# Float16 halves for three sets of float32 products, and a new order of items, in a fused AdaLN layer

## The reference

```
h = layernorm(x) * (1 + ca) + sa
x = x + ga * attn(h)     # rmsnorm, in_w, gate; two branches:
                         #   a: 4-tap depthwise conv, two low-rank maps (A, Bm), ha
                         #   b: 9-tap depthwise conv, silu, pw, hb
                         #   y = gate * fuse([a, b]); out_w; + residual
h = layernorm(x) * (1 + cb) + sb
x = x + gb * moe(h)      # 160 experts of width 64, top 8 by sigmoid, plus a shared expert
shared = silu(h @ w_gate_shared.T) @ w_down_shared.T
```

## Time and profile before

| | us |
|---|---|
| Median of 3 runs | 523.34 (523.1 to 523.37) |
| Profiled execution | 523.24 |
| its span | 521.5 |
| PE busy | 506.1 (97%) |
| DVE busy | 493.2 (95%) |
| ACT busy | 422.2 (81%) |
| POOL busy | 24.9 (5%) |

### The profile page before, as it was taken

How to read it: one execution, slowest core, us unless ns; L and a number is a source line. 1 busy time by engine, 2 the same in 40 slices (tenths; PEclk the granted TensorE clock), 3 DMA queues, 4 the chain that set the end, 5 groups by cost and what they waited for, 6 DMA issues and landing times.

```text
span 521.5 us, 7182 instructions
## 1 busy us (share of the span) xinstructions
PE 506.1 (97%) x2416; PEld 244.3 (47%) x2416; DVE 493.2 (95%) x637; ACT 422.2 (81%) x690; POOL 24.9 (5%) x45
## 2 busy tenths in 40 slices
PE   7897899999999999999999999999999999999996
PEld 5543444544454444444554444444454444444442
DVE  6999999999999999999999999998999989999995
ACT  6588998889989977877999877884799877877773
POOL 6211001001000000000200000000100000000000
PEclk9998999999999999999999999999999999999999
DMA  7797364556664765565354656564465766666650
GB/s 267 256 366 294 128 216 166 162 173 203 194 190 155 239 190 196 183 215 178 129 195 147 239 179 203 188 212 140 162 202 160 223 205 206 204 207 205 209 165 20
DMA packets 33165, 101.30 MB, mean 194 GB/s; under 512 B 3684, under 2 KB 8936, under 8 KB 33128
## 3 DMA queue, kind: packets, MB, share of 16 engines
q1 hardware_dynamic: 33128, 100.84, 58.9%
...
## 4 chain that ended last, share of the span: by engine, by line
PE 87%; DVE 5%; ACT 2%; DMA 2%; issue 2%; SPq 1%; ACTq 0%; DVEq 0%
PE bank L1158 27%; PE bank L1159 27%; PE bank L1160 27%; PE bank L1304 2%; DMA idf<-idf_dram 1%; PE bank L1314 1%; DMA mod<-rows_mod 1%; DVE w L953 1%; PE bank L1403 1%; SPq L551 0%; PE bank L1169 0%; ACT s_all L809 0%; PE bank L1426 0%; PE bank L1324 0%; PE bank L1201 0%
## 5 line engine op out<-in xcount | busy, mean ns | idle before, releaser
L809 ACT ACTIVATE s_all<-bank 128x512 f32<-128x512 f32 x320 | 188.9, 594 | 70.3 <-PE bank L1160 69.0
L1118 DVE TENSOR_TENSOR g_all<-s_all,g_all 128x1024 f16<-128x1024 f32 x160 | 195.7, 1223 | 13.6 <-ACT g_all L828 13.3
L1129 DVE TENSOR_TENSOR s_all<-s_all,c_all 128x1024 f32<-128x1024 f32 x158 | 193.1, 1222 | 0.0
L828 ACT ACTIVATE g_all<-s_all 128x1024 f16<-128x1024 f32 x160 | 168.2, 1051 | 1.1 <-DVE s_all L1129 1.1
L1158 PE MATMUL bank<-g_all,w 128*128 128x512 f16 x320 | 121.3, 379 | 0.7 <-DVE g_all L1118 0.7
L1158 PE MATMUL bank<-x_h,w 128*128 128x512 f16 x320 | 121.3, 379 | 0.6 <-ACT s_all L809 0.5
L1159 PE MATMUL bank<-g_all,w 128*128 128x512 f16 x320 | 121.3, 379 | 0.0
L1160 PE MATMUL bank<-g_all,w 128*128 128x512 f16 x320 | 121.3, 379 | 0.0
L1160 PE MATMUL bank<-x_l,w 128*128 128x512 f16 x320 | 121.3, 379 | 0.0
L1159 PE MATMUL bank<-x_h,w 128*128 128x512 f16 x320 | 121.3, 379 | 0.0
L1158 PEld LDWEIGHTS bank<-g_all,w 128*128 128x128 f16 x320 | 31.3, 98 | 40.0 <-DVE g_all L1118 2.8
...
## 6 DMA issues: line engine op xcount, KB each, us to landing
...
```

The source lines that it names most:

```text
L809: a(sr[J % SRING][:, q * L:(q + 1) * L], U[q][:], ACT.Silu, scale=1.0 / ES).then_inc(s["s_done"], 1)
L828: a(gh[n % GRING], sr[n % SRING], ACT.Copy).then_inc(s["hi_set"], 1)
L1118: e.tensor_tensor(gl[n % GRING], sr[n % SRING], gh[n % GRING], ALU.subtract).then_inc(s["lo_set"], 1)
L1129: e.tensor_tensor(sr[J % SRING], sr[J % SRING], cr[J % CRING], ALU.mult).then_inc(s["gm"], 1)
```

## The change

Three things are changed.

1. The shared down product takes float16 pairs. The weights `sdw` become `sdw_h` and `sdw_l`, laid out with the 64 rows twice instead of padded by zeros. The silu result `ss32` (now its 64 rows twice, since the shared up weights stand twice) goes to `ssx`: its high half everywhere (item `ssh`, ACT), then in the second 64 rows the low half (item `ssl`, DVE). Two float16 matmuls give the product: high and low weights, each by `ssx`.
2. In chunks 2 and 3 (`YB16 = 2`), yb0 and yb1 use pairs of `wb` (items `wbh` on ACT, `wbl` on DVE, once) and of `s32` (`sxh` on ACT, `sxl` on DVE, once a chunk), with `split`.
3. `walk` and `WITH` have a new order. Several semaphores are merged into others with higher counts; they wait for the same events.

```
-                        mm(Y[:], sdw[:], ss32[:], start=True, stop=False).then_inc(s["sd_ps"], 1)
+                        pe.wait_ge(s["ssl_set"], c + 1)
+                        mm(Y[:], sdw_h[:], ssx[:], start=True, stop=False)
+                        mm(Y[:], sdw_l[:], ssx[:], start=False, stop=False).then_inc(s["sd_ps"], 1)

                     for i in range(ML):
+                        if c >= YB16:
+                            w = slice(q * P, (q + 1) * P)
+                            last = split((A1, A2)[q][:], (wb_h[:, i, w], wb_l[:, i, w]), (sx_h[:, i, :], sx_l[:, i, :]),
+                                         start=False, stop=(i == ML - 1))
+                            continue

+                elif n == "ssh":
+                    act.wait_ge(s["ss_set"], c + 1)
+                    a(ssx[:], ss32[:], ACT.Copy).then_inc(s["ssh_set"], 1)
+                elif n == "sxh":
+                    act.wait_ge(s["s_set"], c * ML + ML)
...
+                    a(sx_h[:], s32, ACT.Copy).then_inc(s["sxh_set"], 1)
+                elif n == "wbh":
+                    act.wait_ge(s["wb_set"], 1)
+                    a(wb_h[:], wb[:], ACT.Copy).then_inc(s["wbh_set"], 1)

+                elif n == "ssl":
+                    dve.wait_ge(s["ssh_set"], c + 1)
+                    e.tensor_tensor(ssx[INTER:], ss32[INTER:], ssx[INTER:], ALU.subtract).then_inc(s["ssl_set"], 1)
+                elif n == "wbl":
+                    dve.wait_ge(s["wbh_set"], 1)
+                    e.tensor_tensor(wb_l[:], wb[:], wb_h[:], ALU.subtract).then_inc(s["wbl_set"], 1)
+                elif n == "sxl":
+                    dve.wait_ge(s["sxh_set"], c - YB16 + 1)
+                    e.tensor_tensor(sx_l[:], s32, sx_h[:], ALU.subtract).then_inc(s["sxl_set"], 1)
+                    e.scalar_tensor_tensor(out=sdw_l[:], in0=sdf[:], scalar=YS, in1=sdw_h[:], op0=ALU.mult,
+                                           op1=ALU.subtract).then_inc(s["sdw_set"], 1)
```

491 lines of the change are left out of this document (246 added, 245 removed), and 27 rows, old and new, of the table WITH.

## The result

The changed kernel took 526.98 us (median of 6, 525.0 to 528.78), the kernel before beside it 523.25 (523.09 to 523.37): ratio 1.0059, 95% interval 1.0043 to 1.0075. It is slower by 3.7 us. Forecast was 520.6, the range ended at 524.1. The profiled execution of the changed kernel took 528.78, the longest of its six; its span is 527.0.

The account below looks back on a forecast made before the run. The prediction took PE's work to bound the kernel from 60 to 509 us. From 523.24, less 4.07 of PE work (3.42 products, 0.65 moved ya0), plus 0.4 start and 1.0 holes, it forecast 520.6 us, range 518.2 to 524.1.

Parts of the forecast that it names:

- The products (3.42): PE saves 1.72 us on four shared down products and 1.70 on weight products of chunks 2 and 3.
- DVE still fits, but its lead over PE in these duos shrinks from 9.7 to 3.1 us: Duos 0 to 119: PE's count falls from 350.0 to 344.9 us, DVE's rises from 340.3 to 341.8.
- DVE becomes the bound: Rival, chance 0.08: DVE, full from 60 to 340 us, can't hide 1.56 us more and PE's saving is lost; 524.8.
- The rule set against the start-to-start count: Skill page: the next DVE operation waits for an empty pipeline, so DVE would have only 0.9 us of air in 280.
- The holes (+1.0): New PE waits: 0.6 in duos 0 to 9, 0.7 at chunk 2's halves, less 0.3 at chunk 3's table load.
- The start (+0.4): Start of the duos: 3.92 us more in DVE's queue up to chunk 0's normalised weights, less waits that go.
- together 3.3 to 3.8: DVE's waits before chunk 0's normalised weights that would go: some 2.7 at the first turn, plus those for mod and x_h.
- the order costs its count: Rival, chance 0.10: all 3.9 us added to DVE's queue delay the start; 524.1.
- Interval of 346 to 347: Sign: chunk 0's to chunk 3's shared down product, 351.0 us before, falls to 346 to 347 with 5.3 less PE work.
- Turn of weights at 55.5 to 56.5: Sign: chunk 0's turn of weights starts at 55.5 to 56.5 us.
- PE's waits below 1.5 us in 60 to 340: Sign: PE waits less than 1.5 us in the stretch from 60 to 340 us.
- DVE low of chunk 0 before 16.5: Sign: DVE's low item of chunk 0 starts before 16.5 us, at about 15.7 to 16.3 instead of 17.97.

Follow-up runs that it names:

- after_again: The changed kernel run and profiled once more with nothing edited: 525.38 us, ratio 1.0041 to the kernel before.
- new_order_f32: The kernel before with the changed kernel's walk and WITH, old float32 products, the six new items left out: 527.65 us, ratio 1.0090.
- before_padded: The kernel before plus nine 128x512 DVE operations that nobody waits for, spread over chunks 0 to 3: 525.63 us, ratio 1.0063.
- rms_gap: The changed kernel plus four one-column DVE operations behind the mean square of chunks 2 and 3: 522.86 us, ratio 0.9992 to the kernel before.
- late_ssh: rms_gap with chunk 0's ssh moved behind the second pair of spread weights on ACT: 522.73 us, ratio 0.9992 to the kernel before.
- early_wbh: late_ssh with wbh on ACT moved from duo 30 to duo 22: 522.81 us, ratio 0.9998 to the kernel before.

## Why the prediction was wrong, point by point

**The products (3.42).** Mechanism and size were right as PE's work: 32 float32 records of weight products became 16 and 24 float16 ones, the tail behind chunk 3's product fell by 0.43 as counted, and I2 by 2.20 (after_again) for a count of 1.28 (the rest, by the table of work, is items that the order moved and waits that went). In one and the same order the set gave 2.3 us of time, and 2.52 of the 3.42 behind the second duo (new_order_f32 against after_again): the tail gave its 0.43, I2 1.22 of 1.28, I1 1.03 of 1.28 (no surer than its 0.8), and I0 became 0.16 longer where 0.43 less was counted. On DVE the half of 64 partitions took 0.72 us from start to start at three of its four places, where 0.60 was priced.

**DVE's cover.** The step that failed first is "DVE still fits, but its lead over PE in these duos shrinks from 9.7 to 3.1 us". The 9.7 were PE's sum less DVE's over duos 0 to 119, and of DVE's waits 8.3 us lie in I2, behind 340. In I0 and I1, where nearly all of the added work stands, there were 2.5. The rival "DVE becomes the bound" had the right mechanism with too small a chance (0.08), and it was turned down with just that sum. before_padded shows it without any of the change: 2.22 us for 2.4 in I1, 0 for 1.8 in I2. In the changed kernel without POOL's hole (rms_gap), the way from the second duo to the end is 2.02 us shorter, not 3.07: the work of PE fell nearly as counted (by 3.9, forecast 4.07), but its waits rose by 1.9 where 1.0 was forecast: by 1.2 in I0 and 1.1 in I1 (0.6 there in late_ssh), less 0.4 elsewhere. In I0 DVE's work (114.2) now passes PE's (113.7), in I1 the two are level (116.7 and 116.9).

The rule set against the start-to-start count was told only in half. The Trainium skill, page VectorE: DVE Perf Modes, section "The DRAIN you can't avoid", goes on that a next operation that is not held starts earlier; with that part the starts in the earlier trace rows agree (1.14 us apart where 1.25 is recorded). And its warning, next to no air in DVE from 60 to 340 us, came nearer to what before_padded measured than the 9.7 did.

**The holes (+1.0).** Those I named came small: PE's excess at the weight products of chunk 2 was 0.19 us (forecast 0.7), in duos 0 to 9 0.3 (0.6), and the 0.48 behind the table load of the earlier trace rows went away (0.3 forecast). At chunk 1's table loads (I0) a hole of 0.68 us came that I had not named and that the kernel before has not; of the 1.3 of PE's waits in rms_gap's I0 it is the largest. The one that cost 2.7 to 3.0 I did not name either. The change moves `rms` of chunk 2 from behind duo 9 to behind duo 11, and I had written that POOL's queue keeps its order, so nothing was to be paid. I had read no duration of POOL at all, nor asked what runs on DVE beside it; in the trace of before the powers in the duos are recorded with 1.91 us against 1.01 for one alone, which was the sign. Price by rms_gap: 2.5 us of time, 2.9 of I0.

**The start (+0.4).** The second duo began 4.61 us later in the first profile, 2.27 in the second. The count of DVE's queue, 3.92, was nearly right: up to the normalised weights DVE's own work went from 48.4 us (54.78 less 6.40 of waits over 0.1) to 51.7 (58.24 less 6.51), and lies from 51.8 to 52.0 in the other profiled kernels that have all of it ahead. What failed is the gain against it, "together 3.3 to 3.8": the waits that I saw in the earlier trace rows did go, but others came. Up to the normalised weights DVE's waits over 0.1 us are 4.6 to 7.2 (mean 5.9) in five profiles of the old order and 4.0 to 6.5 (mean 5.2) in five of the new, so 0.7 was gained. Chunk 0's low half started at 18.31, not by 16.5, and DVE waited at the first matrices:

```profile
7.93 0.35 DVE L920 TENSOR_SCALAR s_all<-s_all,vec 128x256 f32<-128x256 f32 x1 [2.45 <-DMA s_all<-mats_dram]
```

for 0.68 us before. That transfer varies by itself (0.36 to 2.45 in the profiled kernels of either order). Five profiled executions of the old order have the second duo at 58.2 to 60.6, mean 59.3; five of the new order with all of it ahead at 61.9 to 64.2, mean 62.9: 3.7 us. Of these, 2.6 lie up to the weights. The other 1.1 is a path that I had not looked at: from the weights to the second duo it takes 5.97 us for 4.82 (5.46 in new_order_f32, which has no ssh, and in late_ssh). ACT has ssh and duo 0's silus in front of the spreads, since duo 0's up products now come right before the turn of the weights, in place of PE's wait of 1.41:

```profile
61.02 0.63 PE L1422 MATMUL bank<-idf,h 128*128 128x128 f32 x4 [0.74 <-ACT h L823]
...
63.29 0.63 PE L1422 MATMUL bank<-idf,x 128*128 128x128 f32 x4 [1.19 <-ACT x L823]
```

A wait in front of an instruction was treated as slack to be filled; what filled it delayed ACT. In the first profile the clock adds to it: from 10.5 to 20.6 us of the span it was at 0.50, 1.2 in place of 2.4 GHz, where the kernel before has 0.83 on average over the same stretch (columns as in the earlier trace rows).

```profile
10.50:20.60 10.10, 9.67 (x41) 8.46 (x41) 9.73 (x34) 5.61 (x18) 4.14 (x2) 0.50 1.03 380
```

The second profile has neither (its transfer took 0.82), so the two are the likely reason why the first profile's second duo is 2.3 us later, though no run parts them. So the rival "the order costs its count" (0.10) had the start's mechanism. That its 3.9 is near the profiles' 3.7 is in part luck: DVE's count gave 2.6 of it, ACT's path the rest.

**The signs named.** Interval of 346 to 347: 350.99, or 348.03 without POOL's hole. Turn of weights at 55.5 to 56.5: 59.21. PE's waits below 1.5 us in 60 to 340: 3.3 recorded for L1203 on ACT alone. "DVE low of chunk 0 before 16.5": 18.31. "Wrong if the second duo starts after 62": 64.21. Each of these pointed the right way. The other sign of being wrong, waits of PE on DVE's low halves through 60 to 340, did not come as such: PE's recorded waits there are for ACT: at 107.30 behind POOL's power, at 158.25 (0.67) behind chunk 1's table loads, at 308.71 where ACT had itself waited 1.00 us for a low half of DVE.

**The sum.** For after_again: 523.24 + 2.27 (start) + 0.01 (from there: -3.07 forecast, 2.03 of POOL's hole by rms_gap's profile, and 1.05 of further waits of PE) = 525.52, its profiled time. As one profile differs from the next by up to 0.8 in I1, the last two parts are known no better than that.

**What stays open.** By these parts rms_gap ought to be 1.5 us slower than the kernel before (start 3.5, rest -2.0), and its profile is (522.9 against 521.5). Its median is 0.5 us faster. The profiled run was the slowest of its 12, and the start varies by 2 to 3 us between profiles of the same order. The part behind the second duo varies less (459.83, 459.69 and 459.78 us in rms_gap, late_ssh and early_wbh; 462.78 and 461.86 in the two of the changed kernel). An estimate from this: take from each median the 1.75 us around the span and the profiled part behind the second duo, and the start is left. It comes out at 59.3 to 60.3 us for the five kernels of the old order and at 61.3 to 62.5 for the five of the new, 2.1 us later on average and not 3.7; rms_gap's is 61.3, so 1.5 later, less 2.0 behind it, which gives its -0.5. That the unprofiled runs take as long behind the second duo as the profiled one is assumed in it, not shown. Why the same four short operations let POOL in at one place and not always at the other stays open too.
